# A transformer block on one core: the first stage's q, k and v from two fp32r parts in three products, its norm on ScalarE

## What is computed

```python
mod = (_silu(L0_c) @ L0_wmod).reshape(L0_c.shape[0], 6, 1, -1)
sa, ca, ga, sb, cb, gb = (mod[:, i] for i in range(6))
h = _layernorm(x, axis=-1) * (1 + ca) + sa
qkv = h @ w_qkv                      # 256 -> 3 * 256
q, k, v = heads(qkv)                 # 16 heads of 16
q, k = apply_rope(q), apply_rope(k)
a = softmax(causal(q @ k.T * 16 ** -0.5)) @ v
x = x + ga * (a @ w_proj + b_proj)
h = _layernorm(x, axis=-1) * (1 + cb) + sb
x = x + gb * ffn(h)                  # router, 2 of 8 experts, shared expert
```

## Time and profile before

| | us |
|---|---|
| three runs | 3307.47, 3312.66, 3314.26 |
| median | 3312.66 |
| profiled execution | 3308.82 |
| its span | 3307.1 |

### The profile page before, as it was taken

One profiled execution on the slowest core, in us unless ns is written; L12 is line 12 of the kernel. 1 busy time (PEld: TensorE's weight loads), 2 busy tenths in 40 slices (PEclk: granted clock), 3 DMA queues, 4 the chain that ended last, 5 costly groups with the idle time before them and its releaser, 6 DMA issues. The chain is left out here.

```text
span 3307.1 us, 61435 instructions
## 1 busy us (share of the span) xinstructions
PE 2912.5 (88%) x22508; PEld 1616.0 (49%) x22508; DVE 2518.0 (76%) x4678; ACT 1588.5 (48%) x2160; POOL 884.5 (27%) x1100
## 2 busy tenths in 40 slices
PE   6885699999999999999999996873999999788888
PEld 3553133333333333333333325763888888677776
DVE  5885989888898888898888914664777777566665
ACT  2542166666676666666666782221444444111111
POOL 5773010111110111101111112664222222333332
PEclk8997699999999999999999997775999999899999
DMA  4776111122111212111221005664444455332332
GB/s 132 204 209 186 49 35 47 48 54 53 43 44 49 54 48 57 38 46 48 55 52 43 20 8 160 212 198 167 155 155 155 156 159 156 105 94 85 96 97 73
DMA packets 388533, 317.93 MB, mean 96 GB/s; under 512 B 112720, under 2 KB 374844, under 8 KB 388288
## 3 DMA queue, kind: packets, MB, share of 16 engines
q1 hardware_dynamic: 370752, 277.67, 29.4%
q0 software_dynamic: 12288, 33.57, 3.0%
q10 hardware_dynamic: 5248, 3.41, 0.4%
HBM read 196.89 MB, written 116.93 MB: 95 GB/s over the span
## 5 line engine op out<-in xcount | busy, mean ns | idle before, releaser
L903 ACT ACTIVATE probs<-ps_s 128x1024 f32<-128x1024 f32 (+3 forms) x1280 | 1077.9, 896 | 599.2 <-PE ps_s L1071 598.6
L926 DVE TENSOR_REDUCE piece_rest<-ps_m 128x1 f32<-128x512 f32 (+2 forms) x1260 | 748.8, 646 | 91.8 <-PE ps_m L1046 42.0
L1071 PE MATMUL ps_s<-q_st,k_st 50*128 50x512 bf16 (+7 forms) x5120 | 594.4, 346 | 19.0 <-ACT probs L903 15.2
L1086 PE MATMUL ps_o<-probs,vs 128*32 128x512 f32 (+3 forms) x5120 | 600.8, 541 | 4.3 <-POOL probs L883 1.2
L883 POOL TENSOR_SCALAR_AFFINE_SELECT probs<-probs 128x256 f32<-128x256 f32 x512 | 204.9, 406 | 1481.2 <-ACT probs L903 1476.0
L926 DVE TENSOR_REDUCE piece_late<-ps_m 128x1 f32<-128x512 f32 x900 | 548.8, 666 | 33.0 <-PE ps_m L1038 17.9
L1038 PE MATMUL ps_m<-k_st,q_st 48*128 48x512 bf16 (+3 forms) x2400 | 407.5, 353 | 65.8 <-DVE piece_rest L926 48.1
L1038 PEld LDWEIGHTS ps_m<-k_st,q_st 48*128 48x128 bf16 x2400 | 106.9, 93 | 651.8 <-DVE piece_rest L926 339.0
L1071 PEld LDWEIGHTS ps_s<-q_st,k_st 50*128 50x128 bf16 (+1 forms) x5120 | 224.1, 95 | 250.8 <-ACT probs L903 91.0
L1803 ACT ACTIVATE act_g<-ps_g 128x512 f32<-128x512 f32 x117 | 69.9, 597 | 279.5 <-PE ps_u L1895 279.5
L1840 DVE TENSOR_TENSOR hid_f<-act_g,ps_u 128x512 f32<-128x512 f32 x117 | 80.5, 688 | 126.8 <-ACT act_g L1803 126.8
(11 more groups left out here) (228 smaller groups left out, 5103.2 us busy)
## 6 DMA issues: line engine op xcount, KB each, us to landing
k_st<-qk_parts SPq DMA_DIRECT2D x768, 32.0 KB, 1.8
qk_parts<-parts SPq DMA_DIRECT2D x124, 192.0 KB, 2.9
q_st<-qk_parts SPq DMA_DIRECT2D x720, 32.0 KB, 1.8
x_r<-expert_rows SPq DMA_DIRECT2D x39, 512.0 KB, 4.6
expert_made<-made SPq DMA_DIRECT2D x39, 512.0 KB, 2.9
x_in<-in_L_attn_x_dram SPq DMA_DIRECT2D x32, 512.0 KB, 4.7
vs<-v_ones SPq DMA_DIRECT2D x64, 256.0 KB, 3.7
v_ones<-v_out SPq DMA_DIRECT2D x60, 256.0 KB, 4.7
```

Source lines behind the costliest of these rows:

```text
L903: act.activation(probs[:, u % PSLOTS, 2 * pair:2 * pair + 2, j * P:ST], ps_s[:, pair, :, j * P:ST], ACT.Exp, scale=SCALE).then_inc(exp_don ...
L926: v.tensor_reduce(dst, ps_m[:, bank, 0:n * w].rearrange("p (n w) -> p n w", n=n), AX.X, ALU.max) \
L1071: last = pe.matmul(ps_s[:, pair, z, j * P:ST], k_st[rows, slot, half, pair, kc * P:(kc + 1) * P], q_st[rows, slot, half, pair, qt * ST + j ...
L1086: last = pe.matmul(ps_o[h * VW:(h + 1) * VW, j * P:ST], vs[:, slot, kc, h * VW:(h + 1) * VW], probs[:, u % PSLOTS, h, j * P:ST], start=(kc ...
```

## The change

- **Products.** The modulated rows and `w_qkv` come in two fp32r parts, and each product of L621 and L624 becomes three: high x high, low x high and high x low (twelve products a tile).
- **Weights.** They are loaded into `w_raw` in the set-up; ScalarE writes the high part there (one copy of 128x1536) and GpSimd the low part (one subtraction of 128x1536), behind its fills.
- **Norm.** `xn` moves from VectorE to ScalarE, as x times `rstd` plus `shift`, at t = 1, behind `v_out`. VectorE makes `shift` (128x4). `xn` has one buffer by unit instead of two, so the power on GpSimd waits until ScalarE has read the old `rstd`.
- **Modulation.** ScalarE writes each half of the modulated rows twice, as fp32r `h_high` and as f32 `h_f`; VectorE subtracts them into `h_low`, half 0 at t = 2 behind `rest`, half 1 at t = 3 between `rope` and `rest`. The products of tile 0 wait for both.
- **Order.** The statistics of the next unit go ahead of `rope` of tile 0, variance and power ahead of `add` of tile 0, and the transposes of `xn` from t = 2 to t = 1.
- **Other stages.** The increments of `held` go from the middle stage (on GpSimd ahead of the variance and of the scatter, on VectorE ahead of `bn_aggr` and `max_index`) and from the last stage (two on GpSimd in `gather`).

```diff
                 Q = dict(
...
                     sin=first.enter_context(nc.sbuf_tensor("sin", [P, NT, HD], F32)),
-                    wqkv=first.enter_context(nc.sbuf_tensor("wqkv", [P, DC, 3 * D], F32)),
+                    wqkv=[first.enter_context(nc.sbuf_tensor(f"wqkv_{part}", [P, DC, 3 * D], F32R)) for part in PARTS],
+                    w_raw=first.enter_context(nc.sbuf_tensor("wqkv_raw", [P, DC, 3 * D], F32)),
                     x_in=first.enter_context(nc.sbuf_tensor("x_in", [P, SPB, TPS, D], F32)),
...
                     consts=first.enter_context(nc.semaphore("p0_consts")),
...
             for u in range(SPB - 1):
...
                     .then_inc(Q["x_loaded"][u], 16)
-            sp.dma_start(Q["wqkv"][:, :, :], w_qkv.rearrange("(c p) n -> p c n", p=P)).then_inc(Q["consts"], 16)
+            sp.dma_start(Q["w_raw"][:, :, :], w_qkv.rearrange("(c p) n -> p c n", p=P)).then_inc(Q["consts"], 16)
             sp.dma_start(Q["cos"][:, :, :], cos_dram).then_inc(Q["consts"], 16)
...
             sp.wait_ge(masks, 2)
...
                     pool.wait_ge(masks, 2 + 2 * slot + z)
...
                     pool.memset(ones.rearrange("p a t -> p (a t)"), 1.0).then_inc(masks, 1)
+            pool.wait_ge(masks, 6)
+            pool.wait_ge(exp_done, 2)
+            pool.tensor_tensor(Q["wqkv"][1][:, :, :], Q["w_raw"][:, :, :], Q["wqkv"][0][:, :, :], ALU.subtract)
 
...
             act.activation(c_exp[:, :], c_row[:, :], ACT.Exp, scale=-1.0).then_inc(exp_done, 1)
+            act.wait_ge(Q["consts"], 16 * 3)
+            act.activation(Q["wqkv"][0][:, :, :], Q["w_raw"][:, :, :], ACT.Copy).then_inc(exp_done, 1)
 
...
         def _(v):
...
         var = sb("var", [P, TPS])
...
         power = sb("power", [P, TPS])
-        xn = sb("xn", [P, 2, TPS, D])
-        h_t = sb("h_t", [P, 2, DC, ST])
+        xn = sb("xn", [P, TPS, D])
+        h_p = [sb(f"h_{part}", [P, 2, DC, ST], F32R) for part in PARTS]
+        h_f = sb("h_f", [P, DC, ST])
+        shift = sb("shift1", [P, TPS])
         rot_c = sb("rot_c", [P, TPS, QK])
...
         qk = sb("qk", [P, TPS, QK])
...
         xn_done = sem("p1_xn")
...
         ht_done = sem("p1_ht")
+        shift_done = sem("p1_shift")
+        h_low = sem("p1_h_low")
         qk_done = sem("p1_qk")
...
         rope_done = sem("p1_rope")
...
                 stand_alone(pool, held)
...
                 pool.wait_ge(pool_own, u + 3)
+                if not (isinstance(u, int) and u == 0):
+                    pool.wait_ge(xn_done, u * TPS)
+                    stand_alone(pool, held)
                 pool.tensor_tensor(rstd[:, :], var[:, :], power[:, :], ALU.pow).then_inc(rstd_done, 1)
...
             def add(u, t):
...
 
...
                 for t in range(TPS):
+                    if t == 0 and more:
+                        rstds(b * SPB + s + 1)
                     if tile(t, 0):
                         add(b * SPB + s, t)
-                    if t == 0 and more:
-                        rstds(b * SPB + s + 1)
                     if tile(t, 3):
...
                         third(u, tt, slot)
...
             v.sem_inc(x_read, SPB)
...
             v.sem_inc(rest_done, 2)
+            v.sem_inc(h_low, DC)
 
...
                 v.wait_ge(x_loaded[slot], turn * 16)
...
                     last = v.bn_aggr(mv[:, t, :], stats[:, t, :])
...
 
-            def normalise(u, slot, x_slot):
+            def shifts(u):
                 v.wait_ge(rstd_done, u + 1)
-                for t in range(TPS):
-                    ins = v.tensor_scalar(xn[:, slot, t, :], x_in[:, x_slot, t, :], mv[:, t, 0:1], rstd[:, t:t + 1],
-                                          ALU.subtract, ALU.mult)
-                    ins.then_inc(xn_done, 1)
-                v.wait_ge(xn_done, (u + 1) * TPS)
-                v.sem_inc(x_read, 1)
+                v.scalar_tensor_tensor(shift[:, :], mv[:, :, 0], -1.0, rstd[:, :], ALU.mult, ALU.mult) \
+                    .then_inc(shift_done, 1)
+
+            def low_rows(u, slot, c):
+                v.wait_ge(ht_done, u * DC + (c + 1 + 2))
+                v.tensor_tensor(h_p[1][:, slot, c, :], h_f[:, c, :], h_p[0][:, slot, c, :], ALU.subtract).then_inc(h_low, 1)
 
...
                 n = u * TPS + t
...
 
...
                 for t in range(TPS):
+                    if t == 0 and more:
+                        stat(b * SPB + s + 1, (s + 1) % SPB, b + ((s + 1) // SPB + 1))
+                    if t == 1 and more:
+                        shifts(b * SPB + s + 1)
                     if tile(t, 0):
                         rope(b * SPB + s, t, s * TPS + t)
-                    if t == 0 and more:
-                        stat(b * SPB + s + 1, (s + 1) % SPB, b + ((s + 1) // SPB + 1))
+                    if t == 3 and more:
+                        low_rows(b * SPB + s + 1, (s + 1) % 2, 1)
                     if tile(t, 3):
...
                         leave(u, tt, slot)
-                    if t == 1 and more:
-                        normalise(b * SPB + s + 1, (s + 1) % 2, (s + 1) % SPB)
+                    if t == 2 and more:
+                        low_rows(b * SPB + s + 1, (s + 1) % 2, 0)
 
...
             steps_of(run, v)
...
             def modulate(u, slot, b):
...
                     act.wait_ge(ht_turned, u * DC + (c + 1))
+                    act.wait_ge(h_low, u * DC + (c + 1))
                     stand_alone(act, held)
-                    act.activation(h_t[:, slot, c, :], ps_ht[:, c, :], ACT.Identity,
+                    act.activation(h_p[0][:, slot, c, :], ps_ht[:, c, :], ACT.Identity,
+                                   bias=mod_t[:, M_SA + c, ds(b, 1)], scale=mod_t[:, M_CA + c, ds(b, 1)])
+                    act.activation(h_f[:, c, :], ps_ht[:, c, :], ACT.Identity,
                                    bias=mod_t[:, M_SA + c, ds(b, 1)], scale=mod_t[:, M_CA + c, ds(b, 1)]) \
                         .then_inc(ht_done, 1)
+
+            def normalise(u, slot, x_slot):
+                act.wait_ge(shift_done, u + 1)
+                stand_alone(act, held)
+                for t in range(TPS):
+                    act.activation(xn[:, t, :], x_in[:, x_slot, t, :], ACT.Identity,
+                                   bias=shift[:, t:t + 1], scale=rstd[:, t:t + 1]).then_inc(xn_done, 1)
+                act.wait_ge(xn_done, (u + 1) * TPS)
+                act.sem_inc(x_read, 1)
 
...
                 if t == 0:
...
                         modulate(b * SPB + s + 1, (s + 1) % 2, b + (s + 1) // SPB)
...
                         take_v(b * SPB + s, t, s % 2, b * 2 + (s // 2 + 1))
+                    if t == 1 and more:
+                        normalise(b * SPB + s + 1, (s + 1) % 2, (s + 1) % SPB)
                     if tile(t, 2):
...
                     if tile(t, 3):
...
                     for t in range(TPS):
...
                             pe.wait_ge(xn_done, u * TPS + (t + 1))
-                        last = pe.transpose(ps_ht[:, c, t * P:(t + 1) * P], xn[:, slot, t, c * P:(c + 1) * P], ident[:, :])
+                        last = pe.transpose(ps_ht[:, c, t * P:(t + 1) * P], xn[:, t, c * P:(c + 1) * P], ident[:, :])
                     last.then_inc(ht_turned, 1)
...
                 if t == 0:
-                    pe.wait_ge(ht_done, u * DC + (DC + 2))
+                    pe.wait_ge(h_low, u * DC + 2 * DC)
                 pe.wait_ge(rope_done, n + TPS - 1)
                 pe.wait_ge(v_done, n + 1)
-                for c in range(DC):
-                    pe.matmul(ps_qk[:, t % 2, :], h_t[:, slot, c, t * P:(t + 1) * P], wqkv[:, c, 0:QK],
-                              start=(c == 0), stop=(c == DC - 1))
-                for c in range(DC):
-                    last = pe.matmul(ps_v[:, t % 2, 0:D], h_t[:, slot, c, t * P:(t + 1) * P], wqkv[:, c, QK:3 * D],
-                                     start=(c == 0), stop=(c == DC - 1))
+                terms = [(c, a, b) for c in range(DC) for a, b in PRODUCTS]
+                for k, (c, a, b) in enumerate(terms):
+                    pe.matmul(ps_qk[:, t % 2, :], h_p[a][:, slot, c, t * P:(t + 1) * P], wqkv[b][:, c, 0:QK],
+                              start=(k == 0), stop=(k == len(terms) - 1))
+                for k, (c, a, b) in enumerate(terms):
+                    last = pe.matmul(ps_v[:, t % 2, 0:D], h_p[a][:, slot, c, t * P:(t + 1) * P], wqkv[b][:, c, QK:3 * D],
+                                     start=(k == 0), stop=(k == len(terms) - 1))
                 last.then_inc(qk_done, 1)
...
             def turn_qk(u, t):
...
                     if tile(t, 2):
...
                         turn_qk(u, tt)
-                    if t == 2 and more:
+                    if t == 1 and more:
                         turn_h(b * SPB + s + 1, (s + 1) % 2)
...
-                stand_alone(pool, held)
                 for j in range(TOPK * TPS):
                     pool.indirect_dma_start(rows_dram, bass.IndirectOffsetOnAxis(at[:, rslot, j:j + 1], 0),
...
-                stand_alone(v, held)
```

(1 more changed line is left out.)

5 lines of the change are left out of this document (removed).

## The result

The changed kernel takes 3373.5 us (median of 4 runs, 3369.7 to 3374.2) against 3312.7: ratio 1.0184, interval 1.0166 to 1.0202. That is 61 slower, where 4 were forecast, and outside the range. The profiled execution has a span of 3367.9 and a mean granted clock of 0.933 (before: 3307.1 and 0.944).

A forecast was written before the change was run, and what follows sets the result against it. TensorE was taken to lead the first stage, VectorE and GpSimd close behind. Period +3.9, entry +2.7, exit -2, set-up 0, increments -2 and clock +2 sum to +4.6: 3317 on the median, range 3290 to 3335.

The forecast's parts named there:

- Products: First stage, TensorE: a tile's products shrink from 2.58 to 2.10 us, 31 over 16 units if TensorE alone decided.
- One unit by hand: First stage: the new order laid out across engines gives a period of 15.53 against 15.25, +3.9 over 14 periods.
- Entry: Start of the first stage and unit 0: first P0 at 41.75 instead of 38.95, +2.7 in all.
- Exit: End of the first stage: the stretch from P0 of unit 15 shrinks from 12.7 to about 10.5, -2.
- Set-up: Weight copy and subtraction before the first stage: covered by TensorE's set-up products, 0; without that cover up to 6.
- Clock: First stage: TensorE's longest idle goes from 1.1 to 2.46, causing one fall of the granted clock, +2.
- the rival (one per unit): First stage: the clock falls behind each wait ahead of P0, +50, 3365; chance of several falls 0.16.
- The increments: Middle and last stages: taking them out saves 0.1 each on VectorE, 0 for GpSimd's in the last stage; -2.
- chain opens: First stage: `xn` hidden and lock waits missed, period 13 to 14.7, total 3280 to 3305; chance 0.26.
- more lock waits: First stage: an `h_low` on VectorE caught by a longer GpSimd queue, up to +17, 3325 to 3334; chance 0.14.
- products no shorter: First stage, TensorE: a tile's products stay at 2.58 or more since loading isn't hidden, +7; chance 0.02.

The follow-up runs named there:

- fill: Changed kernel with nine unread products of 128x512 added per unit on TensorE, in its wait for `h_low`: 3353.9 us, ratio 1.014.
- held_back: Changed kernel with the six increments of `held` put back in the middle and last stages: 3333.6 us, ratio 1.007.
- two_back: Changed kernel with only the two increments ahead of GpSimd's indirect transfers put back (scatter, loads of `gather`): 3337.4 us, ratio 1.007.
- sooner3: Changed kernel, first stage reordered (statistics at end of tile 0, `h_low` ahead of the ropes of tiles 2 and 3), increments kept: 3295.4 us, ratio 0.9949.
- inc_dve: Kernel before, without the increments ahead of VectorE's aggregates and `max_index` and ahead of `gather`'s indirect loads: 3322.4 us, ratio 1.004.

## Why the prediction was wrong

*Products: right.* From the first weight load of P2 to that of P3 it is 2.54 (165.76 to 168.30), of which T 0.44: P is 2.10. The Trainium skill's 131 ns (TensorE: Matmul & The Clock Gate, Back-to-back issue gap) doesn't hold for these products; they stand 232 ns apart.

*One unit by hand: right.* The links came as laid out: `xn` 2.06, `h_low` 1.49 (GpSimd's add first) and 0.68, `h_low` 1 seen by TensorE 17.3 behind P0, of which 1.5 is P0 and T at the lower clock; 15.7 at the full clock in fill against 15.53. Only `shift` was mis-sized, 0.87 to 0.96 in the loop instead of 0.16, and ScalarE wasn't ready for it sooner: it cost nothing. The wait ahead of P0 is 2.24 to 2.52 against 2.46. The chain costs 14 x 0.45 = 6 and not 3.9.

*Entry: right.* From the statistics to the first P0 it is 2.7 more (26.14 to 37.94 against 29.86 to 38.95). The first P0 stands at 37.94 and not 41.75 since an operation of the set-up on VectorE, `c_den`, took 0.28 instead of 3.41 in this execution; in eight of the ten experiments with the new stage it took over 3 and the first P0 is at 40.8 to 42.0, so the 24.4 of the stage would more often be 27 to 28 (held_back 327.3, two_back 328.3). *Exit: -0.2 instead of -2*, since the last unit has its fall too (293.6). *Set-up: right*, GpSimd's subtraction ended at 20.46.

*Clock: the first step that failed, a term of the sum put at 2.* "A shorter idle should do it more rarely: one fall in the stage, +2." There are 15, and the period is 1.4 longer by them (17.12 against 15.7 in those units of fill that had none): 20. I had the rival (one per unit) at 0.16 and spoke against it with "all those falls followed idle of 2.9 or more": four falls in another stage, with other work around them, set no lower bound for this one, nor for their own: in the trace of after the last stage has falls behind waits of 2.03 to 2.77. Its price was off as well: 3.6 a fall for 1.5, since the clock is back after P0 and T. That its 3365 lies near the result is chance: 24 came from this stage, 36 from the increments.

*The increments: the second step that failed, and the larger.* "I take -2", with 0 for those on GpSimd. It was +36: +29.4 and +6.5 (40 by held_back, which puts them back). I costed VectorE's by their own duration alone, gave the sum the wrong sign, set those of `gather` at 0 and left the one ahead of the scatter out; no rival had them. What the one ahead of the scatter does is shift a row of eight transfers by 0.5 against VectorE's two long operations; how the one ahead of the loads acts on the waits of the last stage is told at the end. The Trainium skill (SBUF — State Buffer, Who interferes with whom) says that the order of issue decides which of VectorE and GpSimd is blocked; the trace agrees (1.86 behind `scaled`, 0.96 ahead of it). But the page has an operation of this kind (two inputs from SBUF) not hold transfers up, and here it does: the 157 transfers above all end 0.83 to 0.84 behind the end of `scaled`. The measurement decides.

*The other rivals* (chain opens, more lock waits, products no shorter): none of them happened by itself. That the chain can be opened is shown by sooner3; the rival's range of 3280 to 3305 held the 3295, but it needed a new order on all five engines.

The sum as measured, in spans: the 14 periods took 239.66 (53.66 to 293.32) instead of 213.49, +26.2, of which, by fill's 15.7, 20 the clock and 6 the chain; unit 0 -0.6, first P0 -1.0, exit -0.2: 24.4. With 29.4 and 6.5 for the middle and last stages, 1.1 and -0.4 for the two others: 61.

## What to carry to other kernels

A step that costs nothing by its duration can still set when a row of transfers meets another engine's work; when one is taken out, compare that meeting, and look at TensorE's waits in every stage that the edit touches. When a change makes one wait in a loop longer, here from 1.1 to 2.3, price the case in which the clock falls in each turn from rows of this kernel and keep it in the range; here it cost 20, and the shorter products alone would have given 31 at most. Work of the next unit that the next tile needs should not stand on an engine between this unit's last tile and the next one's first: here a rope and an `h_low` did, and TensorE had 2.3 of nothing.

## What the runs showed that I had not expected

- The clock fell in 14 periods behind a wait of 2.24 to 2.52, with narrow transposes ahead of it; the kernel before waited up to 1.1 there and had none. Each fall lasted 3.4 and cost that unit 1.4 to 1.5.
- ScalarE's copies behind eight transposes came up to 2.4 late in 11 of 14 units of the changed kernel's middle stage, and never with a break of 1 us on GpSimd ahead of its fifth transfer. The cause is open; other moments and lengths of the break weren't tried.
- An operation of VectorE with two inputs from SBUF held up an indirect transfer that GpSimd started behind its start, in all 157 cases to 0.83 or 0.84 behind its own end.
- In the last stage the increment ahead of the indirect loads is worth 10 to 13 (inc_dve against before, two_back against after). TensorE's waits ahead of the last products of that stage (`ps_d`) are about as long in total without it, but come in fewer and longer pieces: in the eight traces with it 1 to 4 of them are over 2.0 and the clock falls 1 to 4 times, low stretches at the stage's begin and end aside; in the ten without it, or with it behind the loads, 13 or 14 are over 2.0 and the clock falls 7 to 11 times. Why the waits bunch was not tried.
